# A mixture-of-experts kernel on one core: the first expert tile before the last routing rounds, first weights read in round 32, the early table one operation per unit, and later pads

## The reference

```python
# x is (32, 256, 128): 8192 tokens of width 128
x = x + attention(layernorm(x))          # 8 heads, key width 16, value width 128
x = x + experts(layernorm(x))            # 8 experts, the best 2 for each token

def experts(x):                          # u: 8192 rows
    gates = sigmoid(u @ centroids.T)     # 8 per row, top 2 kept, divided by their sum
    h = gelu(einsum('nd,edf->enf', u, W1) + b1)        # 128 -> 512, exact gelu
    outs = einsum('enf,efd->end', h, W2) + b2          # 512 -> 128
    return einsum('ne,end->nd', gates, outs)
```

## Time and profile before

| | us |
|---|---|
| median of 3 runs | 707.14 (706.84 to 707.73) |
| profiled execution | 707.2 |
| its span | 705.4 |

### The profile page before, as it was taken

The page is one execution under the profiler, slowest core; times in us unless marked ns, Lnnn a source line. Parts: engine busy times, 40 slices in busy tenths (PEclk is TensorE's granted clock), DMA queues, the critical chain, the costliest instruction groups (busy, mean ns, idle before and its releaser), DMA issues.

```text
span 705.4 us, 14432 instructions
## 1 busy us (share of the span) xinstructions
PE 578.7 (82%) x3889; PEld 440.5 (62%) x3889; DVE 523.7 (74%) x1557; ACT 486.6 (69%) x904; POOL 494.2 (70%) x571
## 2 busy tenths in 40 slices
PE   3799998988988989869976888689999999999200
PEld 1566766666666666636644666468888888888200
DVE  7578898988898888888852688457777777777274
ACT  3467878787777787755665887478888888888000
POOL 6434557888888888857886567757788788877700
PEclk9999999999999999979995899899999999999755
DMA  4645545554545645444325567998777778786099
GB/s 118 176 97 153 151 123 159 164 157 136 143 138 162 169 131 155 121 119 121 108 64 163 162 207 212 258 247 263 243 221 246 244 217 246 250 252 198 12 389 324
DMA packets 107570, 127.31 MB, mean 180 GB/s; under 512 B 19950, under 2 KB 86010, under 8 KB 106497
## 3 DMA queue, kind: packets, MB, share of 16 engines
q1 hardware_dynamic: 89600, 105.34, 51.4%
q0 software_dynamic: 9088, 16.94, 7.3%
q10 hardware_dynamic: 8832, 4.46, 2.1%
HBM read 69.26 MB, written 33.72 MB: 146 GB/s over the span
## 4 chain that ended last, share of the span: by engine, by line
PE 38%; POOL 20%; issue 9%; DMA 6%; DVE 6%; ACT 4%; SPq 2%; POOLq 0%; ACTq 0%; DVEq 0%
POOL slots L590 9%; PE ps_max L948 4%; PE ps_max L949 4%; PE ps_max L950 4%; DMA probs<-comb 3%; DMA probs<-slots 3%; PE ps_proj L1001 2%; PE ps_route L993 2%; PE ps_st L948 2%; PE ps_st L949 2%; PE ps_st L950 2%; PE ps_av L851 2%; PE ps_st L833 2%; PE ps_max L821 2%; POOL att_n L600 2%
## 5 line engine op out<-in xcount | busy, mean ns | idle before, releaser
L657 POOL DMA_INDIRECT comb<-probs,gate_row x156 | 179.8, 1152 | 42.9 <-issue 38.9
L1032 DVE TENSOR_REDUCE row_max<-ps_max 128x2 f32<-128x512 f32 x256 | 173.9, 688 | 47.4 <-PE ps_max L821 42.9
L682 ACT ACTIVATE probs<-ps_st 128x512 f32<-128x512 f32 x256 | 146.8, 594 | 57.6 <-PE ps_st L833 55.3
L1257 DVE TENSOR_TENSOR k_stack<-probs,k_stack 128x512 fp32r<-128x512 f32 x156 | 108.1, 693 | 75.1 <-ACT k_stack L783 73.0
L590 POOL DMA_INDIRECT slots<-y_row,slot_idx x128 | 125.5, 980 | 39.2 <-issue 37.6
L821 PE MATMUL ps_max<-k_stack,q_stack 96*128 96x256 f32 x512 | 132.6, 344 | 24.0 <-DVE row_max L1032 22.9
L821 PEld LDWEIGHTS ps_max<-k_stack,q_stack 96*128 96x128 f32 x512 | 81.8, 198 | 71.9 <-DVE row_max L1032 47.0
L833 PE MATMUL ps_st<-q_stack,k_stack 128*128 128x256 f32 x512 | 106.6, 291 | 13.2 <-ACT probs L682 12.8
L833 PEld LDWEIGHTS ps_st<-q_stack,k_stack 128*128 128x128 f32 x512 | 79.6, 192 | 21.3 <-ACT probs L682 19.1
L851 PE MATMUL ps_av<-probs,v_aug 128*32 128x256 f32 x1024 | 70.3, 393 | 0.0
L780 ACT ACTIVATE probs<-ps_st,b_cur 128x512 f32<-128x512 f32 x78 | 53.9, 692 | 23.1 <-DMA b_cur<-b_all 17.5
(11 more groups left out here) (175 smaller groups left out, 1275.2 us busy)
## 6 DMA issues: line engine op xcount, KB each, us to landing
q_stack<-w_split SPq DMA_DIRECT2D x78, 512.0 KB, 4.3
probs<-slots SPq DMA_DIRECT2D x39, 260.0 KB
q_stack<-q_hi SPq DMA_DIRECT2D x64, 128.0 KB, 2.7
k_stack<-k_hi SPq DMA_DIRECT2D x64, 128.0 KB, 3.0
probs<-comb SPq DMA_DIRECT2D x8, 1024.0 KB, 7.8
X<-in_L_attn_x_dram SPq DMA_DIRECT2D x16, 256.0 KB, 3.3
q_stack<-q_lo SPq DMA_DIRECT2D x32, 128.0 KB, 2.7
k_stack<-k_lo SPq DMA_DIRECT2D x32, 128.0 KB, 3.0
```

Source lines behind the costliest of these rows:

```text
L657: pool.indirect_dma_start(comb_rows, bass.IndirectOffsetOnAxis(gate_row[r][:, c, 1:2].bitcast(I32), 0), res[r][:, c * P:(c + 1) * P], None ...
L682: act.activation(probs[slot % 2][:, h, :, :], ps_st[h % 2][:], ACT.Exp, scale=DK ** -0.5).then_inc(exp_done, 1)
L1032: dve.tensor_reduce(row_max[slot % 2][:, sc, 2 * hp:2 * hp + 2], ps_max[k % 2][:], AX.X, ALU.max).then_inc(smax_reduced, 1)
L1257: dve.tensor_tensor(lo, x, hi.bitcast(F32), ALU.subtract).then_inc(s, 1)
```

## The change

Four edits:

1. PE and ACT end their rounds after 33. Units 0 to 4 of round 34 stand in step -1 (on PE before the transposes of tile 0, on ACT behind its copy), units 5 to 7 in step 0 after part 2 of the hidden layer. Rounds 35 to 40 are drained one step later on PE, ACT and DVE (steps 1 to 6), on POOL at the same steps as before. The waits that share the PSUM tile `ps_route` between routing and output transposes are renumbered by one.
2. SP reads the first weights of tiles 0 and 1 at the start of its round 32, and waits there only for `early_ready`, `w1_saved` and `st_ready`; the waits for `w2_saved` and `b_loaded` move to where these are used. `load_y` of tile 0 follows the last `save_split`.
3. The early table has 17 operations, in parts 0 to 14, one part behind each row maximum of rounds 28 and 29. The copy of `fill` to `pad_start` there is dropped.
4. The fixed pad is written in round 4, the eight others in steps 7, 8 and 9 (3, 3, 2), after the wait for `late_ready` in step 7; the same wait in step 10 is dropped.

```diff
-        def periods(eng, body, at=None):
+        def periods(eng, body, end=35):
...
-            for j in range(24, 35):
-                if at and j in at:
-                    at[j]()
+            for j in range(24, end):
                 body(Period(j // 4, j % 4))
...
-                j = 35 + 4 * i + r if self.fixed else -1
-                self.drain = Period(j // 4, j % 4) if 35 <= j <= 40 else None
+                step = 4 * i + r if self.fixed else FFN_TILES
+                self.first, self.start = step == -1, step == 0
+                self.early = self.round(35 + step, 35)
+                self.drain = self.round(34 + step, 35)
+                self.last = self.round(34, 34) if step in (-1, 0) else None
...
+                if t.fixed and t.i == 8 and t.r == 0:
+
+                    sp.wait_ge(early_ready, 1)
+                    sp.wait_ge(w1_saved, 32 * E)
+                    sp.wait_ge(st_ready, 8 * 29)
+                    load_w1(0, 0)
+                    load_w1(1, 1)
+                if t.fixed and t.i == 1 and t.r == 0:
+                    sp.wait_ge(route_const, 7)
+                    sp.dma_start(slots.rearrange("(c p) w -> p c w", p=P)[:, E * REGION // P:, :], pad_rows[:]).then_inc(padded, 16)
...
-            sp.wait_ge(early_ready, 1)
-            sp.wait_ge(b_loaded, 32)
-            sp.wait_ge(w1_saved, 32 * E)
-            sp.wait_ge(w2_saved, 32 * E)
...
-                if t.fixed and step == EARLY_TILES - 2:
-                    sp.wait_ge(late_ready, 1)
...
+                        sp.wait_ge(w2_saved, 32 * E)
                         sp.wait_ge(st_ready, 8 * 30)
...
-                if t.fixed and 6 <= step <= 8:
-                    if step == 6:
+                if t.fixed and 7 <= step <= 9:
+                    if step == 7:
                         sp.wait_ge(late_ready, 1)
...
-                if t.drain:
-                    body(t.drain)
+                if t.early:
+                    body(t.early)
...
+                if t.first:
+                    body(t.last, range(5))
                 hidden(t, 1)
                 hidden(t, 2)
+                if t.start:
+                    body(t.last, range(5, H))
...
+                    if f == 0 and t.first:
+                        body(t.last, range(5))
+                    if f == 2 and t.start:
+                        body(t.last, range(5, 8))
...
                         if t.fixed and n == 0:
+                            pe.wait_ge(filled, B // 2 - 1)
+                        if t.fixed and n == 1:
                             pe.wait_ge(expn_ready, B // 2)
-                        if t.fixed and n == 1:
+                        if t.fixed and n == 2:
                             pe.wait_ge(filled, B // 2)
...
+                    if t.fixed and t.i == 7 and t.r < 2:
+                        early_table(8 * t.r + k)
```

More of the change, by code:

```diff
@@ new lines, in load_y @@
+            def load_y(n, i, r):
+                row = sp.value_load(table[0:1, bass.ds(n, 1), 0:1].rearrange("p a b -> p (a b)"), min_val=0, max_val=E * REGION)
+                if not since(n, 1):
+                    for m in range(2):
+                        for k in range(TOP_K):
+                            sp.wait_ge(scattered[m][k], 64 * EARLY_PAIRS // 2)
+                    sp.wait_ge(av_done, 62)
+                if not since(n, EARLY_TILES + 1) and n == EARLY_TILES:
+                    sp.wait_ge(padded, 16 * (E + 1))
+                    for m in range(2):
+                        for k in range(TOP_K):
+                            sp.wait_ge(scattered[m][k], 64 * B // 4)
+                if since(n, 4):
+                    sp.wait_ge(yT2_psum, n - 3)
+                    sp.wait_ge(gate_row_ready, n - 3)
+                sp.dma_start(y_tile[r], slots[bass.ds(row, SLOTS), :].rearrange("(c p) w -> p c w", p=P)).then_inc(y_loaded[r], 16)
@@ new lines, in early_table @@
+                made_all()
+                if part == 0:
+                    made_by(dve.tensor_tensor(total[:], fill[:], region[:], ALU.subtract))
+                if part == 1:
+                    made_by(dve.tensor_scalar(tiles_i[:, 0, :], total[:], 0.0, None, ALU.add))
+                if part == 2:
+                    made_by(dve.tensor_scalar(tiles_i[:, 1, :], tiles_i[:, 0, :], SLOTS.bit_length() - 1, None, ALU.arith_shift_right))
+                if part == 3:
+                    made_by(dve.tensor_copy(tiles_f[:], tiles_i[:, 1, :]))
@@ new lines, in early_table @@
+                if part == 7:
+                    made_by(dve.tensor_reduce(tile_start[:, 0:n], passed_end[:, 0:n, :], AX.X, ALU.max))
+                    made_by(dve.tensor_scalar(table[:, 0:n, 1], tile_e[:, 0:n], float(E - 1), None, ALU.min))
+                if part == 8:
+                    made_by(dve.tensor_tensor(tile_k[:, 0:n], tile_n[:, 0:n], tile_start[:, 0:n], ALU.subtract))
+                if part == 9:
+                    made_by(dve.tensor_scalar(tile_start[:, 0:n], tile_e[:, 0:n], float(REGION), None, ALU.mult))
@@ new lines, in early_table @@
+                if part == 10:
+                    made_by(dve.scalar_tensor_tensor(out=tile_row[:, 0:n], in0=tile_k[:, 0:n], scalar=float(SLOTS),
+                                                     in1=tile_start[:, 0:n], op0=ALU.mult, op1=ALU.add))
+                if part == 11:
+                    made_by(dve.tensor_scalar(table[:, 0:n, 0], tile_row[:, 0:n], float(E * REGION), None, ALU.min))
+                if part == 12:
+                    made_by(dve.tensor_tensor(done[:], tiles_f[:], tiles_end[:], ALU.subtract))
@@ L1223, in late_table @@
+                if part == 13:
+                    made_by(dve.tensor_scalar(done[:], done[:], float(n), 0.0, ALU.add, ALU.max))
+                if part == 14:
+                    dve.tensor_tensor(done[:], done[:], tiles_f[:], ALU.min).then_inc(early_ready, 1)
             def late_table(part):
```

95 lines of the change are left out of this document (39 added, 56 removed).

## The result

| | before | after |
|---|---|---|
| median, us | 707.47 (19 runs) | 702.82 (19 runs) |
| profiled execution, us | 707.2 | 704.07 |
| its span, us | 705.4 | 702.3 |

The ratio is 0.9934, with a 95% interval of 0.9919 to 0.9949: 4.7 us faster, a third of the 14 us forecast, and outside the range of 688 to 699.5. The profiled execution is 1.3 us slower than the median, so the traces differ by only 3.1 us. Over the runs after, time and mean granted clock go together: the fastest (698.9) has 0.954, the slowest (706.1) 0.934, the profiled one 0.944.

What follows compares the result with a forecast made beforehand. POOL was taken to bound the late rounds and PE the steady steps, the change touching three breaks: 707.2 - 6.1 (table) - 8.5 (first tile) + 0.6 (pads) = 693.2 us, range 688 to 699.5.

Steps and rivals of the forecast that it cites:

- The first weights' reads: In round 32, 1 MB of weights read while SP only waits for POOL, claimed to cost nothing.
- The table's price: Rounds 28 and 29: POOL's 7.4 us gap goes, 1.3 us come back through DVE; net gain 6.1 us, 3.6 to 7.4.
- a rival in which all 17 draw it: Lock between DVE and POOL: each table operation takes 1.19 us, making the kernel slower, 710.3 us; chance 0.03.
- The first tile ahead: Seam between rounds and steps: tile 0's rows asked for behind the last save, tiles one step further; gain 8.5 us, 5 to 10.
- The pads: Steps 7 to 9: the moved pads lose 11.5 us (8 to 15) against 10.9 before, so 0.6 us lost.
- The three waits: Waits of the pads: a sum over 15 us or under 6 would show the prediction wrong.
- the pads hold back more: Tile 12's new wait at the end of step 9 makes step 11 later: 3 to 5 us more, 697; chance 0.2.
- rounds 28 and 29: Sign for the spread early table: these rounds last about 9.1 us each.
- DVE's 17 operations: Early table in rounds 28 and 29: 0.19 us each taken; an average over 0.35 would show the prediction wrong.
- PE's longest wait for a row maximum: Sign in rounds 28 and 29: this wait stays under 1.5 us.
- The transposes of tile 0: Sign at the seam: they stand 6 to 7 us before the transposes of pair 14.
- The lower clock: Steps 0 to 2: the clock staying at the lower level there would show the prediction wrong.

Runs made afterwards that it cites:

- b_table: The kernel before with only the early table spread over rounds 28 and 29; 704.38 us, ratio 0.9951.
- b_w1: The kernel before with only the two first-weight reads moved to the start of SP's round 32; 710.60 us, ratio 1.0037.
- a_w1hold: The changed kernel with the two weight reads of round 32 held until `y_row` of pair 13 is written; 699.21 us, ratio 0.9893 to before.
- a_w1save_2: The changed kernel with the two weight reads behind the last save, ahead of the rows of tile 0; 703.23 us, ratio 0.9936 to before.
- a_hold_block_2: The changed kernel with weight reads held until `y_row` of pair 13 and the early table in one block before round 28; 703.48 us, ratio 0.9927 to before.
- a_pads: The changed kernel with the eight pads back in steps 6 to 8, the fixed one still in round 4; 700.91 us, ratio 0.9915 to before.

## Why the prediction was wrong

**The first weights' reads** are the step that failed most. The prediction had them "in round 32, where SP only waits for POOL, so they cost nothing". SP's time is free there; the DMA engines and what waits for a landing are not. ACT waits for the scatters of each round before it writes the next `y_row`, and with 1 MB of reads beside it a scatter took 5.7 us to land (4.3 in b_table, without them). They cost 2.6 us alone (b_w1) and 2.9 us in the change (a_w1hold). Through that landing they delay `y_row`, the values behind it and with them the row read of tile 0, and in some executions PE stays at the lower clock for long behind its wait. That is the rival I should have had: before, these reads had their place in front of the rows of tile 0, where they cost about as much (a_w1save_2).

**The table's price** was mis-sized. Forecast 6.1 us (3.6 to 7.4), measured 3.5 (b_table, 2.3 to 4.7 by its interval), just under the lower end, and 4.3 us in the trace of the change where the earlier trace rows ends the two rounds (the last product of round 30's routing: 338.26 against 342.56). The step that failed is 0.19 us for each of 17 operations: 14 of them take 0.15 to 0.25, but three meet a POOL operation and take 1.52, 1.08 and 0.52. All together are 5.7 us instead of 3.2, and with that the prediction's own sum gives 7.4 - (5.7 - 1.9) = 3.6, which is what was measured. The prediction had the row that showed it (`tiles_i` at 1.19), and priced it only as a rival in which all 17 draw it. Three of 17 is the middle case that was left out, with `gate_sum` beside them (1.24 us), which took over the place that `tiles_i` had beside `q_lo`. It shows in POOL's new waits of 2.58 and 0.25 us.

**The first tile ahead**, forecast 8.5, comes out at 6.5 to 8 us once its delay is gone: a_hold_block_2 has 5.2 us together with the pads, whose place costs 1.3 to 2.9. That comes from sums of ratios, and I would not trust it to better than 2 us; the traces spread more. At step 8, ahead of the pads, a_hold_block_2 is only 5.0 us before the kernel before (446.6 - 441.6), a_w1hold 13.3, of which 9 to 10 are not the table's. One piece of the term did not come in the change: from the start of tile 0 to the transposes of step 8 the forecast had 65.6 us (438.1 - 372.5) where before took 67.2; the change took 67.2 (441.20 - 374.04), and a_w1hold 66.2.

**The pads** were forecast to lose 11.5 us, 0.6 more than before. The trace has 13.1, 2.2 more, and the reverse edit gave back 1.3 us (unresolved) and 2.9 us. The mechanism was right: tile 12's row read waits for the pads, and the transposes of step 11 waited 3.6 us (4 to 7 said). The three waits sum to 9.3 us, within the 6 to 15 named, but 3.8 us more are lost behind them, in part at the lower clock: its mean is 0.82 and 0.79 in the stretches behind the first and the third wait (windows after, columns as above):

```profile
452.40:461.64 9.24, 8.20 (x32) 6.41 (x32) 6.14 (x13) 5.55 (x9) 7.33 (x8) 0.82 1.10 285
...
471.83:479.85 8.02, 8.02 (x33) 6.56 (x34) 3.98 (x8) 5.85 (x10) 3.50 (x6) 0.79 0.73 206
```

The rival "the pads hold back more" had this mechanism, at 3 to 5 us.

Of the other signs: rounds 28 and 29 were to last 9.1 us each and took 13.3 and 9.6 (first row maximum to first row maximum on DVE, at about 306.9, 320.2 and 329.7). Three of the four long operations, `gate_sum` among them, ended in round 28. DVE's 17 operations average 0.34 us, just under the 0.35 that would have spoken against the prediction. PE's longest wait for a row maximum was 1.1 us (under 1.5, as said), and the first weights were issued 12.8 us before the last save's start at 358.75 (15 said). The transposes of tile 0 stood 6.8 us before those of pair 14 (378.23 - 371.43, 6 to 7 said), the order of things was as planned. The lower clock was named as a sign for steps 0 to 2; there the mean is 0.84, 0.91 and 0.74 (375 to 383, to 393 and to 403 us), and the long low stretch came in rounds 32 and 33. Of the rivals, that of the pads and a small part of that of the lock came true; for the reads there was none.

In sum: of the 9.3 us missing, 2.9 are the weight reads, 2.6 the table, 0.7 to 2.3 the pads (1.3 to 2.9 less the 0.6 forecast), and the 1.5 to 3 left lie in the first tile's term or in scatter; which of the two, no run parts.

## What to carry to other kernels

Moving a read into a stretch in which its queue is idle is not free if something waits there for the landing of another DMA: look for the engine that waits for landings in that stretch, and hold the read until its last one is in. Small VectorE operations spread between others should be put where GpSimd issues DMAs, not where it does long tensor arithmetic, and those that cannot be are to be counted one by one. Where a wait of TensorE can drop its clock, the slow stretch behind it is to be priced beside the wait, as a range: here it was worth 6 us in one execution and some 1.5 in another with a longer wait. A write that gates a later read is best placed at least one step ahead of that read.

## What the hardware showed that I had not expected

- The last of a scatter's four indirect DMAs landed 5.7 us after its issue with two reads of 512 KB beside it (the change and b_w1), 6.8 in a_pads, and 4.3 and 4.2 without them (b_table, a_hold_block_2). With the reads held, ACT never waited over 1.71 us for a landing in rounds 32 and 33 (a_hold_block_2).
- PE's granted clock fell to half behind a wait of 3.3 us in a stretch that was otherwise full, and stayed there for over 10 us while PE was busy throughout. With matmuls in the wait it kept the full level, and the stretch behind took 13.5 us instead of 19.5. But before, it also fell behind waits of 0.25 and 0.92 us, for some 3 us, and in a_pads it was back some 6 us after a wait of 4.4.
- A VectorE addition over 128x4 elements took 1.24 us beside a GpSimd operation over 128x512 and 0.16 us before, with GpSimd idle. Beside `rstd`, a GpSimd operation over 128x4 that took 1.04 us, one over 128x96 kept its 0.26 us.
